# Attention's product in 32-column tiles and one semaphore for each of a loop's eight steps, in a recurrent stack on one core

## The reference, cut to what matters

```
x = x + attention(x, cond)      # 16 heads, two keys and values: no-op and cond
x = x + moe(x, cond)            # shared silu unit + 8 experts, top 2, exact gelu
x = x + x @ W_e + u(cond)       # no dependence between time steps
x = x + lstm(x)                 # z = x_t @ Wx + b + h @ Wh, 1024 steps in order
```

## Time and profile before

| What | us |
|---|---|
| Median of 3 runs | 1958.13 |
| Lowest and highest | 1957.75 to 1960.11 |
| The profiled execution's own time | 1957.56 |
| Its span, first to last instruction | 1955.8 |
| TensorE matmuls busy | 1889.5 (97%) |
| TensorE weight loads busy | 1439.8 (74%) |
| VectorE busy | 1390.7 (71%) |
| GpSimd (POOL) busy | 1133.8 (58%) |
| ScalarE busy | 827.2 (42%) |

### The profile page before, as it was taken

The page is one execution under the profiler, slowest core; times in us unless marked ns, Lnnn a source line. Parts: engine busy times, 40 slices in busy tenths (PEclk is TensorE's granted clock), DMA queues, the critical chain, the costliest instruction groups (busy, mean ns, idle before and its releaser), DMA issues.

```text
span 1955.8 us, 256304 instructions
## 1 busy us (share of the span) xinstructions
PE 1889.5 (97%) x113680; PEld 1439.8 (74%) x113680; DVE 1390.7 (71%) x7217; ACT 827.2 (42%) x4757; POOL 1133.8 (58%) x4950
## 2 busy tenths in 40 slices
PE   7999999999999999999999999999999999999998
PEld 5777777777777777777777777777777777777776
DVE  2677777777777777777777777777777777777776
ACT  1344444444444444444444444444444444444444
POOL 4555655655555565565555556555555655665565
PEclk9899999999999999999999999999999999999999
DMA  4000000000000000000000000000000000000000
GB/s 170 4 4 3 3 4 3 3 3 4 3 3 4 3 3 3 4 3 3 4 3 3 4 3 3 3 4 3 3 4 3 3 3 4 3 3 4 3 3 3
DMA packets 57724, 14.67 MB, mean 8 GB/s; under 512 B 56176, under 2 KB 56304, under 8 KB 57200
## 3 DMA queue, kind: packets, MB, share of 16 engines
q1 hardware_dynamic: 57712, 14.50, 3.2%
HBM read 12.37 MB, written 2.10 MB: 7 GB/s over the span
## 4 chain that ended last, share of the span: by engine, by line
PE 87%; ACT 6%; DVE 4%; issue 2%; DMA 0%; POOL 0%; DVEq 0%; SPq 0%; POOLq 0%; ACTq 0%
PE psum L953 29%; PE psum L943 29%; PE psum L815 10%; PE psum L836 7%; PE psum L855 6%; DVE h_ring L703 3%; ACT o_act L532 3%; ACT psum L535 2%; PE psum L798 2%; PE psum L829 2%; PE psum L843 1%; PE psum L892 1%; PE psum L793 0%; DMA wkv_sb<-in_wkv 0%; PE psum L776 0%
## 5 line engine op out<-in xcount | busy, mean ns | idle before, releaser
L943 PEld LDWEIGHTS psum<-wh_sb,h_ring 128*2 128x2 f32 (+1 forms) x32768 | 488.4, 90 | 416.6 <-DVE h_ring L703 409.8
L953 PE MATMUL psum<-h_ring,wh_sb 128*32 128x2 f32 x65536 | 765.7, 173 | 1.8 <-issue 1.8
L953 PEld LDWEIGHTS psum<-h_ring,wh_sb 128*32 128x32 f32 x65536 | 725.8, 109 | 2.0 <-issue 2.0
L943 PE MATMUL psum<-wh_sb,h_ring 128*2 128x64 f32 (+1 forms) x32768 | 656.8, 220 | 50.8 <-DVE h_ring L703 20.2
L526 ACT ACTIVATE f_act<-psum 128x4 f32<-128x4 f32 x1024 | 177.3, 173 | 698.6 <-DVE psum L744 698.6
L744 DVE STREAM_TRANSPOSE psum<-psum 128x64 f32<-128x64 f32 x1024 | 266.1, 260 | 274.6 <-PE psum L943 262.7
L815 PE MATMUL psum<-up_sb,x 128*32 128x256 f32 (+1 forms) x3096 | 311.8, 460 | 0.0
L746 DVE STREAM_TRANSPOSE psum<-psum 128x64 f32<-128x64 f32 x1024 | 271.5, 265 | 1.9 <-PE psum L943 1.9
L703 DVE SCALAR_TENSOR_TENSOR h_ring<-o_act,psum 128x4 f32<-128x4 f32 x1025 | 163.0, 159 | 141.9 <-ACT psum L535 115.9
L836 PE MATMUL psum<-down_e,hid_t 128*16 128x256 f32 x3096 | 251.6, 382 | 0.6 <-ACT down_e L507 0.6
L756 DVE TENSOR_TENSOR_SCAN psum<-addend,psum 128x16 f32<-128x16 f32 x1024 | 199.3, 195 | 52.2 <-ACT psum L529 2.4
(11 more groups left out here) (142 smaller groups left out, 2286.0 us busy)
## 6 DMA issues: line engine op xcount, KB each, us to landing
x_a<-in_x SPq DMA_DIRECT2D x129, 16.0 KB, 1.6
x_s<-in_x SPq DMA_DIRECT2D x129, 16.0 KB, 1.6
up_sb<-in_up SPq DMA_DIRECT2D x1, 2048.0 KB, 12.7
out_y<-y_sb SPq DMA_DIRECT2D x128, 16.0 KB, 1.4
down_sb<-in_down SPq DMA_DIRECT2D x1, 1536.0 KB, 8.3
wx_sb<-in_wx SPq DMA_DIRECT2D x1, 1024.0 KB, 14.5
wh_sb<-in_wh SPq DMA_DIRECT2D x1, 1024.0 KB, 16.6
wkv_sb<-in_wkv SPq DMA_DIRECT2D x1, 512.0 KB, 4.4
```

The source lines that it names most:

```text
L943: last = nc.tensor.matmul(z[32 * j:32 * j + row + B, :], h_ring[:, prev, c, WIN - B - row:WIN], wh_v[:, c, g, j, :], start=False, stop=(c ...
L953: last = nc.tensor.matmul(by_row(z)[32 * j:32 * (j + 1), m, row:row + B], wh_v[:, c, g, j, 32 * m:32 * (m + 1)], h_ring[:, prev, c, WIN - ...
```

## The change

The attention product goes over four tiles of 32 columns for each half instead of two of 64. `hid` becomes eight semaphores, one for each step; `close(slot)` raises the one of the step that follows by 8. TensorE makes its register once an iteration, as t + 8, and all waits of the iteration use it. POOL's wait is written for the first of the eight.

```diff
--- before.py
+++ after.py
@@ -300,7 +300,8 @@
         terms_in = sem("terms_in")
         cell = sem("cell")
         cell_tanh = sem("cell_tanh")
-        hid = sem("hid")
+
+        hid = [sem(f"hid_{u}") for u in range(U)]
         h_read = sem("h_read")
         y_made = sem("y_made")
         y_stored = sem("y_stored")
@@ -350,7 +351,7 @@
         @block.gpsimd
         def _(pool):
             pool.sem_inc(y_stored, 16)
-            for s in (f_made, i_made, o_made, f_turned, a_f, cell, cell_tanh, hid, x_turned, i_based):
+            for s in (f_made, i_made, o_made, f_turned, a_f, cell, cell_tanh, x_turned, i_based, *hid):
                 pool.sem_inc(s, READY)
             pool.sem_inc(terms_in, 2 * READY)
             pool.sem_inc(i_and_c_in, 2 * READY)
@@ -460,7 +461,7 @@
                 gates(i * U + (READY + U), fall[:, :])
                 weigh(i * U + (READY + U)).then_inc(hid_e_out, U)
 
-                pool.wait_ge(hid, i * U + (READY + U + 1))
+                pool.wait_ge(hid[0], i * U + (READY + 2 * U))
                 pool.tensor_tensor(half_h[:].rearrange("p c (u b) -> p u c b", b=B), h_ring[:, :, :, WIN - B:WIN],
                                    half[:, :].unsqueeze(2).unsqueeze(3).to_broadcast([P, U, C, B]),
                                    ALU.mult).then_inc(h_read, U)
@@ -703,7 +704,7 @@
                 nc.vector.scalar_tensor_tensor(out=h_ring[:, slot, :, WIN - B:WIN],
                                                in0=o_act[:, :].rearrange("p (c b) -> p c b", b=B), scalar=1.0,
                                                in1=c_tanh.rearrange("p (c b) -> p c b", b=B),
-                                               op0=ALU.add, op1=ALU.mult).then_inc(hid, 1)
+                                               op0=ALU.add, op1=ALU.mult).then_inc(hid[(slot + 1) % U], U)
 
 
             with dve.Fori(READY, READY + T, U) as t:
@@ -794,8 +795,9 @@
 
             def attend(attn, weights):
                 for c in range(C):
-                    for j in range(0, P, 64):
-                        last = nc.tensor.matmul(attn[j:j + 64, c], value_w[:, c * P + j:c * P + j + 64], weights,
+                    for j in range(J):
+                        last = nc.tensor.matmul(attn[32 * j:32 * (j + 1), c],
+                                                value_w[:, c * P + 32 * j:c * P + 32 * (j + 1)], weights,
                                                 start=True, stop=True, skip_group_check=True)
                 return last
 
@@ -957,11 +959,12 @@
                 return last
 
             with nc.Fori(READY, READY + T, U, engines=(PE_ENGINE,), head_slot={PE_ENGINE: 0}) as t:
+
+                now = pe.snap(t + U)
                 for u in range(U):
                     prev = (u - 1) % U
-                    now = pe.snap(t + (u + 1))
-
-                    pe.wait_ge(hid, now)
+
+                    pe.wait_ge(hid[u], now)
                     recur_row(z_f, GF, u * B, prev).then_inc(f_made, 1)
                     if u == 0:
                         pe.wait_ge(i_based, now)
```

## The result

The changed kernel takes 2006.42 us (median of 4, 2005.13 to 2006.97) against 1958.28 us, a ratio of 1.0243 (95% interval 1.0225 to 1.0261): 48 us slower, where 15 us less were forecast. It lies near the price of the forecast's slow rival, the loop body that outgrows its place, but that is not what happened.

A forecast was written before the change was run, and what follows sets the result against it. The chain through VectorE's close was taken to pace the loop, with TensorE late in step 4; 128 x 0.12 = 15.4 us off 1957.56 gave 1942.2, about 1942.7 as a median, range 1938 to 1949.

The forecast's parts named there:

- the loop body that outgrows its place: Rival: TensorE's loop body stops for instructions each iteration; 1968 to 2032 us, middle 2000; chance 0.06 with pairs beyond 0.49.
- What bounds the kernel: Recurrence loop: the chain through VectorE's close paces steps where TensorE is ready; gains per iteration of 14.85 us repeat 127 times.
- The tiles: Attention's product ahead of step 4: 32-column tiles cut close-to-product from 0.33 to 0.21 us, 0.12 us an iteration gained.
- a drain: Reading of step 4's lateness: the array drains at each change of tile width, idling attention's weight loads 0.43 us each.
- The rival of dear pairs: Attention's 16 load-and-matmul pairs take 0.42 us, so 0.07 us an iteration is saved: 1949.2 us; chance 0.05.
- The eight semaphores: VectorE's close raises one of eight semaphores by 8, adding no wait; lower bound on the gain nothing.
- The seven register instructions: Taken from TensorE's queue ahead of steps 1 to 7; costed at nothing, bound 0.35 us an iteration.
- the counts pay for them: TensorE's loop body: the tiles' matmuls alone would give 1798 instructions; removing seven counts gives 1791, one short of seven blocks.
- The priced case: One stop of 0.80 to 1.31 us at TensorE's loop top, costing 0.2 to 0.7 us an iteration, 25 to 90 us.
- the case that the forecast left unpriced: All seven instruction blocks of TensorE's loop come anew each time; said only to be far more.
- an eighth block should fit as well: Argument against the outgrown body: TensorE holds 2048 instructions in blocks of 256.

The follow-up runs named there:

- e3: The change, but each of the eight semaphores is raised by 1 and TensorE keeps a second count, that of the iteration: 1943.21 us against 1957.96.
- e7: e3 with attention's product back in 64-column tiles: 1956.97 us, ratio 1.0000 to the kernel before.
- e1: The change without its tiles: attention's product in 64-column tiles, eight semaphores raised by 8 and one count: 2011.13 us against 1957.96.
- e4: The kernel before with its one semaphore hid raised by 2, TensorE's counts doubled, 64-column tiles: 2014.65 us, ratio 1.0286.
- e5: The kernel before, with ScalarE's tanh of the transposed gate f raising a_f by 2 in place of 1: 1992.11 us against 1956.66.
- e2: The kernel before with the 32-column tiles alone, TensorE's loop body 1798 instructions: 2455 to 2597 us, median 2513.
- e8: e2 with a branch hint on TensorE's loop, body 1799 instructions: 1945.14 us, ratio 0.9938 to the kernel before.
- e6: e3 with one more register instruction in TensorE's loop, 1793 instead of 1792: 1975, 2002, 2020 and 2101 us, against 1957 for the kernel before.

## Why the prediction was wrong

*What bounds the kernel* held: the chain through the close paces each step but those where TensorE is late, and an iteration repeats 127 or 128 times. This is also why an error of 0.07 us a close became 64 us (2006.4 against 1942.7).

*The tiles* held to the number. Sixteen pairs let TensorE go in time, the drain behind them is gone, step 4's distance fell from 0.33 to 0.21 or 0.22, and e3 came to 1943.21 where the sum said 1942.7. That the old lateness was a drain stays a reading; shown is that the tiles' width alone makes it (e3 against e7). Two details were less good than forecast: in e3 the loads of shape 128*10 have 18.3 us of idle time ahead of them, 0.14 us each and not 0.2, and those of attention keep 16.3 us, 0.13 each. The rival of dear pairs, and the Trainium skill's rule of some 60 cycles for each matmul behind it ("TensorEngine Tiling (Array Packing)", Instruction Overhead), did not show: attention's 16 matmuls started at 1017.96 and their stretch of 0.33 us, less 0.18 us of one (182 ns is the mean of L799's 2064), leaves 0.15 us for the row of starts, L843's value in the earlier trace rows.

*The eight semaphores* are the step that failed. It said: "The bound below is nothing, since no wait is added: VectorE's close signals as often as before, by 8 on one of eight semaphores in place of 1 on one." I counted waits and signals and looked at TensorE's queue alone; I never asked whether the close's instruction can still carry both its wait and its signal. In these kernels it doesn't: on VectorE (e1, e4) and on ScalarE (e5) a rise by more than 1 on an instruction that waits puts that wait into an instruction of its own. It costs 0.07 us a close, where the forecast had nothing: seven of the eight close-to-close intervals grew by 0.06 to 0.08 us (step 4's besides what the tiles took off it, 0.12), and step 6's by 0.01, as TensorE had been 0.07 us late there (0.28 before, 0.21 after). Step 7 had the same lateness to give and yet grew by 0.08: VectorE's transpose of f comes 0.60 us behind the product there (1024.11 to 1024.71), 0.48 in step 3 (1016.51 to 1016.99), because VectorE is still at its own side work. In sum, by the closes on the two timelines, 0.38 us an iteration. The queue instruction itself is recorded with 21 ns; the rest of the 0.07 was not measured apart.

The trace of before held a warning that I read past: the earlier trace rows shows closes with their wait inside, and VectorE's other instructions that rise by 8 (in step 4, for instance) do have wait instructions ahead of them, off the path. It even settles what splits them off. GpSimd's L400 waits for the constant 5 (L399) and raises its semaphore by 8, and the wait stands by itself:

```profile
L399 POOLq EVENT_SEMAPHORE  x130: 17/17/17, 21.0 to 1943.7; - x130
```

L398 waits for a constant too, and L402 against a register (L401); both raise by 1, and neither L397 nor L401 has a queue instruction. So the size of the rise decides, on three engines, and it makes no difference whether the wait is for a constant or against a register.

*The seven register instructions* are worth nothing, as forecast (e7, with six of them gone), and their true use was the one in the forecast's bracket: "the counts pay for them."

*The outgrown loop* was given too small a price and the wrong threshold. The change itself stays below it (1791 instructions, 9 packets), so this rival did not occur, and that its 2000 us lie near the measured 2006 is chance. For a body that does go beyond, 90 us were far too little: e2 costs 497 to 639 us. The priced case was one stop of 0.80 to 1.31 us at the top of each iteration; what e2 shows is the case that the forecast left unpriced, all blocks fetched anew, but in 40 of 128 iterations, at 16 us each. That an eighth block should fit as well, which I took from the Trainium skill's 2048 instructions ("Runtime: NRT & Kernel Launch", Instruction fetch mechanics), is true only with the hint (e8); without it the limit is seven blocks (e3 against e6).

## What to carry to other kernels

On the path that paces a loop, look at each instruction as a unit of wait, work and signal: raising a signal by more than 1 splits off the wait, and the views to check are the queue instructions of the engine (DVEq, ACTq) and the distance from the releaser's start to the start of the released. Signal by 1 there, and let the waiting engine keep a second count. Count the instructions of a long loop body in blocks of 256 before adding any; beyond seven, arm the branch hint (bodies of 1799 to 1815 were run with it, nothing longer), and look at the packets of the instruction queue: a mean over the iterations hides that they come in bursts.

## What the runs showed that I had not expected

- An instruction with a wait and a rise by 2 or 8 has its wait split off: 0.07 us on VectorE (0.19 to 0.26 us from tanh to close), 0.06 us on ScalarE (0.30 to 0.36). On GpSimd the wait is split off too (L399); what it costs there was not measured.
- TensorE's loop body costs nothing at 1792 instructions (10 packets in the run). At 1793 it was fetched anew five times in the run (54 packets, 2020 us; four executions took 1975 to 2101), at 1798 forty times (369 packets, 2597 us; 2455 to 2597), each time in nine blocks of 16 KB and at a cost of some 16 us. With a branch hint a body of 1799 to 1815 costs nothing in the steady state.
- Where TensorE is late anyway, a later close costs nothing: without the tiles the same split cost 0.42 us an iteration instead of 0.49. In step 7 that did not help, because VectorE was at side work of its own.
